# Four heads' scores in one TensorE step in layers 0 and 2 of a four-layer cross-attention kernel

## The reference, cut to what matters

```python
# layer 0: rmsnorm, cross attention with 16 query heads of 64 over 4 key/value heads, residual
q = (xn @ wq.T).reshape(B, S, 4, 4, 64); k = (kvn @ wk.T).reshape(B, T, 4, 64)
scores = einsum('bsgrd,btgd->bgrst', q, k) / 8; probs = softmax(scores); out = probs @ v
# layer 1: 8-bit fake-quantised self attention, then cross attention (16 heads of 16), gated GELU MLP
# layer 2: layernorm, cross attention with 16 heads of 64, ReLU MLP
scores = einsum('bhtd,bhsd->bhts', Q, K) * 64 ** -0.5
# layer 3: causal self attention, then cross attention (16 heads of 16), ReLU MLP
```

## Time and profile before

| what | value |
|---|---|
| median of 3 runs | 5165.88 us (5164.52 to 5167.72) |
| the profiled execution's own time | 5168.09 us |
| its span, first to last instruction | 5166.3 us |
| TensorE matmuls busy | 4838.5 us (94%) |
| VectorE, ScalarE, GpSimd busy | 57%, 55%, 42% |
| mean granted TensorE clock | 0.971 of full speed |

### The profile page before, as it was taken

The page is one execution under the profiler, slowest core; times in us unless marked ns, Lnnn a source line. Parts: engine busy times, 40 slices in busy tenths (PEclk is TensorE's granted clock), DMA queues, the critical chain, the costliest instruction groups (busy, mean ns, idle before and its releaser), DMA issues.

```text
span 5166.3 us, 91631 instructions
## 1 busy us (share of the span) xinstructions
PE 4838.5 (94%) x34496; PEld 3541.4 (69%) x34496; DVE 2968.7 (57%) x6704; ACT 2851.6 (55%) x9051; POOL 2148.0 (42%) x4307
## 2 busy tenths in 40 slices
PE   8999999968787787889999999999999999999998
PEld 5666666656666665666666666666667778877777
DVE  5555555556566656664455445544555676767765
ACT  4555555677888888873333333233333566666664
POOL 2333333477877778771111111111112444444443
PEclk9999999989898988999999999999999999999999
DMA  2000000010000000001000000000001100000000
GB/s 79 20 20 20 22 21 20 17 40 17 14 20 11 20 17 14 17 30 38 13 11 13 14 13 10 13 12 12 13 10 31 35 18 21 18 17 21 18 17 10
DMA packets 40039, 103.09 MB, mean 20 GB/s; under 512 B 4912, under 2 KB 21552, under 8 KB 38192
## 3 DMA queue, kind: packets, MB, share of 16 engines
q1 hardware_dynamic: 39600, 97.23, 6.0%
HBM read 82.53 MB, written 14.68 MB: 19 GB/s over the span
## 4 chain that ended last, share of the span: by engine, by line
PE 80%; ACT 9%; POOL 7%; DVE 2%; issue 2%; DMA 0%; SPq 0%; ACTq 0%; DVEq 0%
PE ring L1268 47%; PE ring L1219 12%; PE score L1200 11%; ACT e L1378 5%; POOL e L1735 4%; PE ring L1250 3%; PE ring L1243 3%; POOL e L1745 2%; PE ring L1257 2%; PE ring L1216 1%; DVE nmax L1513 1%; POOL rsumw L1728 1%; POOL work L1721 1%; ACT probs L1418 1%; PE score L1195 1%
## 5 line engine op out<-in xcount | busy, mean ns | idle before, releaser
L1738 POOL TENSOR_SCALAR e<-e,rsum 112x375 f32<-112x375 f32 (+1 forms) x2048 | 1103.3, 556 | 2678.9 <-DVE rsum L1520 2676.7
L1378 ACT ACTIVATE e<-score,nmax 112x375 f32<-112x375 f32 (+1 forms) x2048 | 1042.5, 536 | 384.9 <-DVE nmax L1513 381.0
L1513 DVE TENSOR_REDUCE nmax<-score 112x2 f32<-112x750 f32 (+1 forms) x1152 | 1079.7, 953 | 301.1 <-PE score L1200 299.8
L1418 ACT COPY probs<-ring 125x336 f32<-125x336 f32 (+1 forms) x976 | 403.8, 448 | 1318.7 <-PE ring L1219 1256.9
L1268 PE MATMUL ring<-h,weights 128*128 128x224 f32 x3840 | 910.0, 370 | 5.8 <-ACT h L1350 2.7
L1219 PEld LDWEIGHTS ring<-consts,e 112*125 112x125 f32 x4608 | 590.7, 188 | 272.3 <-issue 138.6
L1200 PE MATMUL score<-keys,q 64*112 64x375 f32 (+2 forms) x3584 | 619.9, 503 | 162.9 <-ACT e L1378 150.5
L1268 PEld LDWEIGHTS ring<-h,weights 128*128 128x128 f32 x3840 | 707.8, 197 | 89.9 <-issue 24.9
L1219 PE MATMUL ring<-consts,e 112*125 112x112 f32 x4608 | 675.1, 281 | 6.7 <-DVE heads L1604 4.3
L1378 ACT ACTIVATE e<-score,nmaxc,quant 112x375 f32<-112x375 f32 (+1 forms) x1024 | 555.2, 554 | 10.7
L1268 PE MATMUL ring<-weights,ctx 128*125 128x256 f32 (+1 forms) x1536 | 560.6, 495 | 0.1
(11 more groups left out here) (121 smaller groups left out, 5844.4 us busy)
## 6 DMA issues: line engine op xcount, KB each, us to landing
ctx<-ctx_t SPq DMA_DIRECT2D x128, 375.0 KB, 3.0
out_t<-x SPq DMA_DIRECT2D x64, 224.0 KB, 1.9
x<-out_t SPq DMA_DIRECT2D x48, 224.0 KB, 2.5
weights<-weights SPq DMA_DIRECT2D x7, 1024.0 KB, 5.2
x<-x_t SPq DMA_DIRECT2D x16, 224.0 KB, 2.5
weights<-weights SPq DMA_DIRECT2D x1, 3328.0 KB, 10.7
weights<-weights SPq DMA_DIRECT2D x1, 2304.0 KB, 9.1
weights<-weights SPq DMA_DIRECT2D x1, 2048.0 KB, 7.3
```

Source lines behind the costliest of these rows:

```text
L1378: ins = nc.scalar.activation(e_of(u)[:, n * width:(n + 1) * width], score_bank(u)[0:S, n * width:(n + 1) * width], ACT.Exp, bias=minus, sc ...
L1418: ins = nc.scalar.copy(dst, src)
L1513: ins = dve.tensor_reduce(to, src, AX, ALU.max, negate=True)
L1738: ins = nc.gpsimd.tensor_scalar(mine, mine, rsum[0:S, slot(u), n:n + 1], 0.0, ALU.mult, ALU.add)
```

## The change

One line. Layers 0 and 2 join `QUADS`: a step there makes the scores of two neighbouring pairs, eight matmul records in a row, into all four banks, and signals once at the end. The matmuls, their operands and their banks are the same as before. VectorE's maximum and ScalarE's exponentials stay one step for each pair. The planner now sees one score step of 1.66 in the place of two of 0.83, so the order of every engine's list is worked out anew.

```diff
-QUADS = (1, 3)
+QUADS = (0, 1, 2, 3)
```

## The result

The changed kernel takes 5084.39 us (median of 4 runs, 5083.73 to 5085.05) against 5165.2 of before in the same comparison: 80.8 us less, ratio 0.9843 (95% interval 0.9826 to 0.986). The forecast was 5089.

A forecast was written before the change was run, and what follows sets the result against it. TensorE alone was taken to bound layers 0 and 2. From the profiled span, 5166.3 - 81 (fewer score visits) + 4 (added wait) = 5089.3, forecast 5089 us, range about 5070 to 5118.

The forecast's parts named there:

- The bound: Layers 0 and 2: TensorE alone sets the time, busy 61.70 of 61.70 and 104.80 of 104.80 us a stream.
- The price of a visit: TensorE going to the 64-row scores between full-array jobs costs 0.38 us beyond its work; beside a `pv`, 0.19.
- The number of visits: TensorE's visits to the 64-row scores in layers 0 and 2 fall from 496 to 256, so 240 go.
- Which visits go: Layers 0 and 2: depends on the new order; three cases save 91, 81 or 70 us, 81 taken.
- the middle case: Layers 0 and 2: score visits beside `pv` halve with the rest, saving 81 us.
- its first case: Layers 0 and 2: all score visits that go stand between full-array jobs, saving 91 us.
- The added wait: Score steps need all four banks free, waiting also for the pair just before: 4 us, bounds 0 to 19.
- the slack of 2.45 us: Layer 0: two pairs' chain takes 4.98 us, TensorE returns every 7.43, leaving 2.45; nothing waits in layer 2.
- The waits of layer 3: Rival: layer 0's score steps wait for ScalarE as layer 3's do, 19 us, total 5104 to 5115; chance 0.14.
- Nothing gained: Rival: four heads overlap no better than two in the 64-row scores, no gain, 5170 us; chance 0.03.
- The four banks as the bound: Rival: layer 0's score steps need 8.9 us against 7.43, losing 186 us, slower at 5271; chance 0.06.
- The order elsewhere: Rival: new order leaves more visits beside `pv` and a worse layer 1, 70 saved, 17 lost, 5113; chance 0.08.

## Why the prediction was right

**The bound.** The prediction had TensorE alone setting the time in layers 0 and 2. Right: the stretch of layer 2 became 44.5 us shorter with 43.7 us less of TensorE's busy time, and the steady streams of layer 0 still have TensorE busy but for 0.43 us in six of them.

**The price of a visit, 0.38 us.** Right: eight visits fewer in a stream of layer 2 made it 3.03 us shorter, 0.38 each, and put back in at 163 places a visit cost 0.36. The Trainium skill's drain of about 128 cycles ("TensorE: Matmul & The Clock Gate", What happens when you issue a matmul), taken twice for each visit because a change of tiling mode drains the engine ("TensorEngine Tiling (Array Packing)", Key Properties), gives an estimate of 17 us for that test; 58.4 was measured.

**The number of visits.** Right: 16 x 8 in each layer after, 240 and 256 before.

**Which visits go.** Mis-sized: the prediction took the middle case, visits beside `pv` halving, 81 us. What came is its first case, 91 us: 59 visits of layer 0 lay beside a `pv` in TensorE's list before and 63 after, and 46 of layer 2 in both. TensorE's busy time fell by 88.3 us.

**The added wait.** The size was right: 4 us with bounds of 0 and 19 was forecast, and TensorE's time without work rose by 4.1 us in the whole profiled execution, 5.7 of it in layer 0, with a little less elsewhere. The parts were not those of the prediction. The score waits of layer 0 are 6.9 us, but 4.3 of them were there before, so 2.6 are new; another 2.6 stand at the transposes. Score waits in the 13 steady streams were nearly absent, as the slack of 2.45 us said. The prediction also said that layer 0 has no self attention between. Its last stream has, before the change too, and nearly all score waits of the layer lie there. In that last stream the granted clock was 0.91 against 0.95 before, and it became 1.2 us longer where a steady stream became 2.7 us shorter. The waits at the transposes stayed when the four-bank wait was split and went with a new order, which points to the planner's list and not to the banks. So the 4 us were a choice near the low end that met the number, in part by luck.

The sum: the part saved was about 7 us more than forecast (88.3 against 81) and the wait about as forecast, which gives 84.2 us between the two profiled executions. Between the medians it was 80.8, against a forecast of 77. The 3.4 us between these two are the spread of single executions.

**The rivals.** The waits of layer 3: they would have put 19 us of waiting into layer 0; it was 5.7. Nothing gained: excluded by 80.8 us and by the visits put back in. The four banks as the bound: not with four heads, but with pairs the same rule cost 104.7 us, so the mechanism is real. The order elsewhere: layers 1 and 3 kept their steady streams of 81.9 and 71.1 us.

## What to carry to other kernels

Where an engine is busy without a gap, look for the same instruction with two durations and ask what came before it: here each visit to the 64-row scores between full-array jobs cost 0.36 to 0.38 us beyond its work, and the cure was fewer visits, not fewer matmuls. A wait that ends double buffering is judged by what it comes to per visit against the work that the engine can do meanwhile: half as many waits over twice the work added some 5 us without work in layer 0, the same rule on single pairs cost 105 us. Before a wait in the changed kernel is put down to the change, the same stretch of the kernel before has to be read: 4.3 of the 6.9 us of score waits were there already. With an order made by a planner, it is worth looking at the place of single steps for half a microsecond lost in some streams; a due time shifted by 0.3 was worth 11 us.

## What the runs showed of the hardware

A float32 matmul of one column over 128 rows costs 18.0 / 163 = 0.11 us behind full-array work (0.10 in the chain of work). The same over 64 rows, set between two pairs of 64-row matmuls, costs 0.19, and the starts of the two row groups move from 7 ns to about 0.10 us apart; a filler for one group is no neutral control.

After the 2.89 us without work at 948.5 us, TensorE's granted clock fell. Busy time by stretch, changed kernel, during the wait and behind it (the granted clock is the third number from the end):

```profile
948.50:951.40 2.90, 0.07 (x1) 0.00 (x0) 0.00 (x0) 2.90 (x15) 2.81 (x9) 1.00 0.02 6
951.50:954.00 2.50, 2.50 (x11) 1.03 (x12) 0.33 (x2) 0.93 (x2) 2.40 (x8) 0.61 0.00 0
```

A mean of 0.61 is mostly the lower of its two levels, 1.2 GHz, and the eight score records took 2.32 us instead of 1.52. The wait so cost another 0.8 us that no row of waits shows. This is not new with the change. The kernel before shows it behind a wait of 2.08 us in the same stream, busy time by stretch and timeline:

```profile
988.40:990.10 1.70, 1.63 (x5) 0.56 (x5) 0.20 (x1) 1.59 (x6) 1.60 (x5) 0.50 0.00 0
988.47 1.59 PE L1200 MATMUL score<-keys,q 64*112 64x375 f32 x4 [2.08 <-ACT e L1378]
```

Four score records took 1.59 us there, against 0.89 at the full clock.
